# A graph network on one core: the first half of each gate's Wq product moved to the head of the gate, and the gate's end taken bank by bank

## What is computed

```python
def _rgcn(x, W_rel, W_root, bias, src, dst, etype):      # out = x @ W_root + bias
    ...                                                  # + sum over 3 relations of mean(x[src] @ W_rel[r]) by dst
def _gate(h, q, Wg, bg, Wq, bq):
    hg = einsum('bnf,gf->bng', h3, Wg[:, :F]);  qg = einsum('blf,gf->blg', q, Wg[:, F:]) + bg
    attn = sigmoid(hg[:, :, None, :] + qg[:, None, :, :])
    qi = einsum('bnlf,blf->bnf', attn, q)
    alpha = sigmoid(einsum('bnf,gf->bng', h3, Wq[:, :F]) + einsum('bnf,gf->bng', qi, Wq[:, F:]) + bq)
    return alpha * tanh(qi) + (1.0 - alpha) * h3
h = gate(relu(rgcn1(x)));  h = gate(relu(rgcn2(h)));  x = layernorm(x + h)
```

## Time and profile before

| | |
|---|---|
| median of 3 runs | 1258.62 us (1258.33 to 1262.88) |
| the profiled execution | 1258.37 us, its span 1256.6 us |
| PE busy | 1118.9 us, 89% of the span |
| DVE, ACT, POOL busy | 733.8, 548.8, 131.6 us |
| mean granted clock of PE | 0.944 |

### The profile page before, as it was taken

How to read it: one execution, slowest core, us unless ns; L and a number is a source line. 1 busy time by engine, 2 the same in 40 slices (tenths; PEclk the granted TensorE clock), 3 DMA queues, 4 the chain that set the end, 5 groups by cost and what they waited for, 6 DMA issues and landing times. The chain is left out here.

```text
span 1256.6 us, 17142 instructions
## 1 busy us (share of the span) xinstructions
PE 1118.9 (89%) x7246; PEld 921.1 (73%) x7246; DVE 733.8 (58%) x1049; ACT 548.8 (44%) x575; POOL 131.6 (10%) x84
## 2 busy tenths in 40 slices
PE   7999997999879869999579887878999999999986
PEld 6888874445779745448458787854899999999973
DVE  6583447887043158881343464324688888888851
ACT  0221017886032258880123353222566666666630
POOL 2020003554000015550000000000000000000000
PEclk9999997999979989999799888968999999999998
DMA  8044235220323451212224202410877777777720
GB/s 266 1 150 150 76 109 150 61 68 18 118 108 119 136 148 51 66 37 76 76 76 151 76 1 76 173 50 1 272 256 241 248 234 255 233 258 232 257 79 26
DMA packets 82192, 162.66 MB, mean 129 GB/s; under 512 B 4034, under 2 KB 60126, under 8 KB 81822
## 3 DMA queue, kind: packets, MB, share of 16 engines
q1 hardware_dynamic: 80720, 151.86, 36.2%
q0 software_dynamic: 1392, 9.66, 2.9%
HBM read 157.86 MB, written 0.80 MB: 126 GB/s over the span
## 5 line engine op out<-in xcount | busy, mean ns | idle before, releaser
L1533 DVE TENSOR_TENSOR Wlo<-W,Whi 128x2304 fp32r<-128x2304 f32 x68 | 173.7, 2556 | 43.4 <-ACT Whi L1134 43.4
L1134 ACT CAST Whi<-W 128x2304 fp32r<-128x2304 f32 x68 | 144.2, 2122 | 0.0
L851 PE MATMUL PS<-Whi,Mhi 128*128 128x384 f32 x408 | 139.6, 342 | 3.5 <-DVE Mlo L1562 3.5
L618 PE MATMUL PS<-QH,SEL 128*128 128x512 f32 x384 | 118.7, 433 | 23.0 <-DVE QH L1324 15.3
L851 PE MATMUL PS<-Wlo,Mhi 128*128 128x384 f32 x408 | 136.5, 335 | 0.0
L851 PE MATMUL PS<-Whi,Mlo 128*128 128x384 f32 x408 | 136.5, 335 | 0.0
L392 POOL TENSOR_TENSOR PRDP<-arena 128x1024 f32<-128x1024 f32 x48 | 114.5, 2386 | 103.2 <-PE PS L634 83.6
L618 PEld LDWEIGHTS PS<-QH,SEL 128*128 128x128 f32 x384 | 67.4, 195 | 74.2 <-DVE PRD L1348 22.7
L1015 ACT ACTIVATE arena<-PS 128x1024 f32<-128x1024 f32 x96 | 98.5, 1026 | 34.5 <-PE PS L618 34.5
L1015 ACT ACTIVATE PS<-PS 128x1024 f32<-128x1024 f32 x96 | 97.9, 1020 | 0.0
L851 PEld LDWEIGHTS PS<-Whi,Mhi 128*128 128x128 f32 x408 | 76.8, 188 | 8.3 <-DVE Mlo L1562 8.3
(11 more groups left out here) (233 smaller groups left out, 2186.4 us busy)
## 6 DMA issues: line engine op xcount, KB each, us to landing
W<-in_L_rel SPq DMA_DIRECT2D x68, 1152.0 KB, 5.6
W<-in_W_rel SPq DMA_DIRECT2D x6, 2304.0 KB, 8.7
W<-in_W SPq DMA_DIRECT2D x6, 2304.0 KB, 8.4
arena<-in_qU SPq DMA_DIRECT2D x96, 128.0 KB, 2.6
W<-in_WqT SPq DMA_DIRECT2D x4, 2304.0 KB, 9.1
W<-in_W_root SPq DMA_DIRECT2D x2, 2304.0 KB, 14.0
W<-in_WgT SPq DMA_DIRECT2D x2, 2304.0 KB, 8.4
QH<-QH POOLq DMA_DIRECT2D x2, 1536.0 KB, 9.9
```

The lines of the kernel that those rows point to most:

```text
L618: mm = pe.matmul(PS[:, 2 * (c % 3) + b // 2, :], SEL[:, i, :], QH[h][:, u, b:b + 2, :].rearrange("p b f -> p (b f)"), start=True, stop=True)
L851: mm = pe.matmul(PS[:, 4 + s % 2, 0:HALF], MS[a][mb][:, k, j * P:(j + 1) * P], WS[b][w % 3][:, k, :], start=n == 0, stop=n == 17)
L1134: nc.scalar.copy(WS[0][w % 3][:], W[(FIRST34 + r) % 2][:, :, q * HALF:(q + 1) * HALF]).then_inc(w_hi, 1)
L1533: V.tensor_tensor(WS[1][w % 3][:], W[(FIRST34 + r) % 2][:, :, q * HALF:(q + 1) * HALF], WS[0][w % 3][:].bitcast(F32), ALU.subtract).then_i ...
```

## The change

1. PE multiplies hT by Wq's first half right behind `natural3` (and the sort), into banks 0 to 2, while ACT and DVE copy the node rows. ACT copies the result by bank to hqT, in xT's memory; the first two `sums` wait for these copies. After the loop six matmuls with the identity put hqT into banks 3 to 5, and only the product with qiT is left there. SP issues the later queries ahead of m = 9 and 16.
2. Relu, messages, qiT, tanh, sigmoid, multiply, add and the split of hT are done by bank (j = 0, 1, 2), each with its own count; products take the contractions in the order in which the banks come (`ready`).
3. The transposes back to natural form are made in three parts (`turn_part`) in banks 6, 7 and 5: for g = 0 the first inside the last product, the second behind it, the third inside the first product of layer 2. For g = 1 the half statistics follow each addition.
4. ACT and DVE split the first two weight thirds of layer 2 during the gate's last product. qiT gets memory of its own.

```diff
-        alphaT = view(arena, 7936, 1536).rearrange("p (k n) -> p k n", k=KC)
+        alphaT = hqT = xT[:]
...
-                if m in (8, 15):
+                if m in (9, 16):
...
                     for k in range(KC):
+                        if ready and m == 0 and k % 2 == 0:
+                            ready(k // 2)
...
+                    if bank_sem and m in (1, 3):
+                        mm.then_inc(bank_sem, 1)
...
+                    for ks in ((0, 1, 2, 3), (4, 5)) if q == 0 else (range(KC),):
+                        for c in range(2):
+                            for k in ks:
+                                if q == 0 and c == 0 and k % 2 == 0:
+                                    if p == 0:
+                                        pe.wait_ge(hs_ready, k // 2 + 1)
+                                    else:
+                                        pe.wait_ge(mt_copied, 3 * (R3 + p - 1) + k // 2 + 1)
...
-                    pe.wait_ge(mt_copied, 3 * (n + 1))
...
-                pe.wait_ge(relu_done, g + 1)
...
-                natural3(hT, W[(m0 + 4) % 2], bank=3, first=True, last=True).then_inc(w_used, 1)
+                natural3(hT, W[(m0 + 4) % 2], bank=3, first=True, last=True,
+                         ready=lambda j: pe.wait_ge(relu_done, 3 * g + j + 1)).then_inc(w_used, 1)
                 if g == 0:
                     sort_edges()
+                weights(m0 + 5)
+                turned_product(0, hT, W[(m0 + 5) % 2], bank_sem=hq_done).then_inc(w_used, 1)
...
+                    if c < 2:
+                        pe.wait_ge(hq_copied, 3 * g + 2 + c)
...
+                for m in range(KC):
+                    pe.matmul(PS[:, 3 + m // 2, (m % 2) * NODES:(m % 2 + 1) * NODES], ident[:], hqT[:, m, :],
+                              start=m % 2 == 0, stop=False, skip_group_check=True)
                 pe.wait_ge(qi_copied, UNITS * (g + 1))
                 to_turned(0, qiN).then_inc(qi_turned, 1)
-                weights(m0 + 5)
-                turned_product(3, hT, W[(m0 + 5) % 2], last=False).then_inc(w_used, 1)
-                pe.wait_ge(qiT_copied, g + 1)
                 weights(m0 + 6)
-                turned_product(3, qiT, W[(m0 + 6) % 2], first=False).then_inc(w_used, 1)
-                pe.wait_ge(gate_done, g + 1)
-                to_natural(0, hT).then_inc(h_turned, 1)
...
+                turned_product(3, qiT, W[(m0 + 6) % 2], first=False, between=first_part, bank_sem=aq_done,
+                               ready=lambda j: pe.wait_ge(qiT_copied, 3 * g + j + 1)).then_inc(w_used, 1)
+                pe.wait_ge(gate_part, 3 * g + 2)
+                turn_part(1).then_inc(part_turned, 1)
+                if g == 1:
+                    pe.wait_ge(gate_part, 6)
+                    turn_part(2).then_inc(part_turned, 1)
...
+                for j in range(3):
+                    if j < 2:
+                        act.wait_ge(hq_done, 2 * g + j + 1)
+                    else:
+                        act.wait_ge(w_used, 7 * g + 7)
+                    nc.scalar.copy(hqT[:, 2 * j:2 * j + 2, :], PS[:, j, :].rearrange("p (k n) -> p k n", k=2)).then_inc(hq_copied, 1)
...
+                if g == 0:
+                    third_hi_turned(0)
+                    third_hi_turned(1)
...
+                    if g == 0:
+                        act.wait_ge(gate_part, j + 1)
+                        nc.scalar.copy(TS[0][:, 2 * j:2 * j + 2, :], hT[:, 2 * j:2 * j + 2, :]).then_inc(hs_hi, 1)
...
                     third_lo_turned(0)
                     third_lo_turned(1)
+                for j in range(3):
+                    ks = slice(2 * j, 2 * j + 2)
+                    dve.wait_ge(alpha_done, 3 * g + j + 1)
+                    then(V.tensor_tensor(tanhT[:, ks], tanhT[:, ks], alphaT[:, ks], ALU.mult))
+                    V.tensor_tensor(hT[:, ks, :], hT[:, ks, :], tanhT[:, ks], ALU.add).then_inc(gate_part, 1)
+                    if g == 0:
+                        dve.wait_ge(hs_hi, j + 1)
+                        V.tensor_tensor(TS[1][:, ks, :], hT[:, ks, :], TS[0][:, ks, :].bitcast(F32), ALU.subtract).then_inc(hs_ready, 1)
...
+                    dve.wait_ge(part_turned, 3)
+                    for t in range(NT):
+                        then(V.tensor_tensor(xN[:, t, 0:512], PS[:, 6 + t, :], xN[:, t, 0:512], ALU.add))
+                        V.bn_stats(stats[:, t, 0, :], xN[:, t, 0:HALF])
```

More of the change, by code:

```diff
@@ L138, in build @@
         QD = [view(arena, 12032 + 1024 * i, 1024) for i in range(2)]
[L139 to L140 removed]
+        qiT, tanhT = put("qiT", [P, KC, NODES], F32, 100)[:], MT[0][:]
+        alphaT = hqT = xT[:]
         qiN = hN
@@ L412, in natural, with turned_product @@
                 return mm
-            def turned_product(bank, T, Wm, first=True, last=True, between=None):
+            def turned_product(bank, T, Wm, first=True, last=True, between=None, ready=None, bank_sem=None):
                 for m in range(KC):
@@ L464, in spread_counts, with natural3 @@
                 mm.then_inc(deg_spread, 1)
-            def natural3(T, Wm, bank=0, first=False, last=False, tiles=range(NT), thirds=range(3)):
+            def natural3(T, Wm, bank=0, first=False, last=False, tiles=range(NT), thirds=range(3), ready=None):
                 for t in tiles:
@@ L472, in natural3 @@
                         for k in range(KC):
+                            if ready and at == 0 and k % 2 == 0:
+                                ready(k // 2)
                             mm = pe.matmul(out, T[:, k, t * P:(t + 1) * P], Wm[:, k, q * THIRD:(q + 1) * THIRD],
@@ L533, in split_product @@
                     pe.wait_ge(wl_ready, w + 1)
[L534 to L538, removed]
+                    for ks in ((0, 1, 2, 3), (4, 5)) if q == 0 else (range(KC),):
[6 more added lines that the diff above has]
+                                        pe.wait_ge(mt_copied, 3 * (R3 + p - 1) + k // 2 + 1)
+                                for a, b in ((0, 0), (1, 0), (0, 1)):
+                                    mm = pe.matmul(PS[:, q, c * NODES:(c + 1) * NODES], WL[b][w % 2][:, k, c, :], TS[a][:, k, :],
+                                                   start=p == 0 and k == 0 and a == b == 0 and c == 0,
+                                                   stop=p == R3 and k == KC - 1 and b == 1 and c == 1, skip_group_check=True)
                     mm.then_inc(wl_used, 1)
+                    if q == 0 and after_first:
+                        after_first()
             for g in range(2):
@@ L992, in _ @@
                     act.wait_ge(small_in, SMALL)
[L993 to L998, removed]
+                    act.wait_ge(rows_looked, EC // 2)
+                for j in range(3):
+                    if g:
+                        act.wait_ge(wl_used, 3 * R3 + j + 1)
+                    elif j < 2:
+                        act.wait_ge(bank_done, j + 1)
+                    else:
+                        act.wait_ge(w_used, 5)
+                    for m in (2 * j, 2 * j + 1):
+                        ins = nc.scalar.activation(hT[:, m, :], PS[:, j, (m % 2) * NODES:(m % 2 + 1) * NODES], ACT.Relu,
+                                                   bias=biasT[:, g, m:m + 1])
+                    ins.then_inc(relu_done, 1)
                 act.wait_ge(w_used, 7 * g + 6)
@@ L1371, in _ @@
-                if g == 0:
-                    ins.then_inc(hN_ready, 1)
+                for j in range(3):
+                    V.tensor_copy(qiT[:, 2 * j:2 * j + 2, :], PS[:, j, :].rearrange("p (k n) -> p k n", k=2)).then_inc(qiT_copied, 1)
+                for j in range(3):
+                    ks = slice(2 * j, 2 * j + 2)
+                    dve.wait_ge(tanh_done, 3 * g + j + 1)
+                    then(V.tensor_tensor(tanhT[:, ks], tanhT[:, ks], hT[:, ks, :], ALU.subtract))
+                if g == 0:
@@ new lines, in _ @@
+                rest = PS[:, 5, :].rearrange("p (t f) -> p t f", t=NT)
+                if g == 0:
+                    dve.wait_ge(part_turned, 1)
+                    for t in range(NT):
+                        V.tensor_copy(hN[:, t, 0:512], PS[:, 6 + t, :])
+                    dve.wait_ge(part_turned, 2)
+                    V.tensor_copy(hN[:, :, 512:FEAT], rest).then_inc(hN_ready, 1)
+                else:
+                    dve.wait_ge(part_turned, 3)
+                    for t in range(NT):
+                        then(V.tensor_tensor(xN[:, t, 0:512], PS[:, 6 + t, :], xN[:, t, 0:512], ALU.add))
+                        V.bn_stats(stats[:, t, 0, :], xN[:, t, 0:HALF])
+                    dve.wait_ge(part_turned, 4)
+                    then(V.tensor_tensor(xN[:, :, 512:FEAT], rest, xN[:, :, 512:FEAT], ALU.add))
+                    for t in range(NT):
+                        ins = V.bn_stats(stats[:, t, 1, :], xN[:, t, HALF:FEAT])
+                    then(ins)
```

85 lines of the change are left out of this document (39 added, 46 removed).

## The result

Four runs of the changed kernel took 1214.09 to 1222.06 us, median 1218.04, against 1260.75 (1258.33 to 1266.79, four runs) of the kernel before: ratio 0.9654, 95% interval 0.9625 to 0.9684. The profiled execution took 1219.05 us with a span of 1217.3, so 39.3 us less span than before, where 43.4 were forecast. PE is as long busy as before (1118.9 us before, 1118.6 after), with the twelve identity matmuls more; what went is time in which it stood still, and some in which it ran at the low clock.

What follows compares the result with a forecast made beforehand. It took the touched stages to be bound by TensorE plus the places where it stands still, with the low clock behind idle time. Its terms summed to -43.4 us, from 1258.4 to 1215.0 us, range 1208 to 1227.

Steps and rivals of the forecast that it cites:

- (a): Layer 1: relation products started bank by bank hide three 0.68 us waits for the last message copy; -2.0 us.
- (b): Gate 1: relu by bank removes the 2.45 us wait before the node product; -2.5 us.
- (c): Head of gate 1: first-half product +9.0, exposed table load +0.7, warm loop start -1.7; +8.0 us in all.
- (i): Head of gate 2: first-half product +7.0, earlier first sigmoid -0.5, faster loop start -0.95; +5.6 us in all.
- (d): Gate ends: six identity matmuls put hqT back into the accumulators; +2.1 us per gate, 4.2 in all.
- (e): Gate ends, qi transposes to end of products: 31.1 us becomes 16.9; -14.2 us per gate, 28.4 in all.
- (f): Gate 1, end of products to layer 2's first aggregation: 28.3 us becomes 14.3, with a 0.35 us wait; -14.0 us.
- (j): End of gate 2, end of products to aggregate of row statistics: 12.83 us becomes 6.7; -6.1 us.
- the first: Rival: weight conversions become the bound at the gate's end and in layer 2; +7 us, 1222 us; chance 0.14.
- The second: Rival: a head does not absorb the product, weights or node rows late; up to 8.67 us lost, 1224; chance 0.08.
- The third: Rival: better than the sum, identity matmuls at transposes' pace and less start-up in the loops; 1209 us; chance 0.06.
- the fourth: Rival: low clock in the gate loop, one loop some 100 us longer; 1315 us; chance 0.03.

Runs made afterwards that it cites:

- p2: Changed kernel with whole waits in the two layers (message copies, layer product before relu, relu before node product); 1229.75 us, ratio to before 0.9758.
- p5: Changed kernel with added matmuls nobody reads where PE idles at the start of both gate loops; 1215.15 us, ratio to before 0.9661.
- p6: Changed kernel with six unread matmuls between gate 2's last transposes and the transposes ahead of the GCN block; 1216.60 us, ratio to before 0.9652.
- p10: Changed kernel with early table load, unread matmuls at loop starts and gate 2's end, and hqT added by DVE; 1206.32 us, ratio to before 0.9584.
- p1: Changed kernel with Wq's first-half product back behind the loop, steps by bank kept; 1235.78 us, ratio to before 0.9798.
- p4: Changed kernel with a one-column sigmoid ahead of gate 1's hqT copies, loading the activation table early; 1220.25 us, ratio to before 0.9667.
- p7: Changed kernel without the six identity matmuls, DVE adding hqT to each bank instead; 1215.67 us, ratio to before 0.9648.
- p8: Changed kernel with the first-half product back behind the loop and layer 2's first two weight thirds converted behind the gate's parts; 1236.13 us, single run.
- p3: Changed kernel with whole waits at the gates' ends, same pieces (qiT copies, sigmoids, parts, transposes, split of hT); 1235.10 us, ratio to before 0.9804.
- p9: Changed kernel with whole waits both in the two layers and at the gates' ends; 1248.55 us, ratio to before 0.9903.

## Why the prediction was right, and where it was off

The forecast was 1215.0 with a range of 1208 to 1227; measured 1218.04. The sum of -43.4 stands against -39.3 in the spans. Two pieces of the table cover several terms, since a whole relu or a set of six sigmoids ends later by itself than a last pair (1.46 us).

- (a), (b), layer 1 by bank: -4.5 forecast, -4.9 measured (4.14 + 0.72). With whole waits (p2) the first comes back as 4.17; of the 2.29 in the second some 1.6 are a cold start that the kernel before didn't have there.
- (c), (i), the product at the heads: +9.7 and +6.5 to the first sigmoid forecast (15.7 less the idle time, with the table load in one and not in the other), +9.61 and +6.13 measured.
- (c), (i), the loop's start: **this step failed.** "In return PE comes warm into the loop: 8.8 instead of 10.49" gave -1.7 and -0.95; measured -0.38 and +0.51. PE did come warm, but the loop's own first waits let the clock fall. The gain of 1.7 and 1.6 was there, as p5 shows, where added matmuls kept the clock up. I had taken the idle time ahead of the loop for the only cause of the low clock in it.
- (d), (e), gate ends: +2.1 - 14.2 forecast, -12.1 a gate; measured 39.17 to 25.74, -13.43, of which 1.46 are the shorter last set: -12.0, in both gates.
- (f): -14.0 forecast, -12.46 - 1.46 = -13.9 measured. The one wait foreseen, 0.35 us, was 0.45 (the prediction's terms for part 3, 0.85 + 2 x 0.73 + 0.63 + 0.73, make 3.67 and not the 3.75 it gives, so 0.27 by its own sum).
- (g), (h), layer 2: -8.2 forecast, -6.46 - 2.76 = -9.2 measured. The waits of 1.40 were worth 1.67 each (aggregations 19.81 us apart before, 18.14 or 18.13 after).
- (j): -6.1 forecast, -5.03 - 1.46 = -6.5 measured.
- Not in the sum: +2.2 us of the GCN product, which started cold; p6 and p10 show it to be the clock. It was cold in all seven kernels with the gate's end by bank and no matmuls added there (the changed one, p1, p2, p4, p5, p7, p8: 23.7 to 24.5 us to its end) and warm before and in p3 and p9, which have whole waits there (21.98 or 21.99). So it comes with the steps by bank and takes 2.2 back from them; why the clock is still low there is not shown. And +0.83 at the start of the kernel, ahead of the change, a matter of the run.

So 2.8 us at the loops' starts, 2.2 at the GCN block and 0.8 at the front were missed, and 1.7 gained in small parts, which brought the sum nearer than its terms were. Of the rivals, the first did not come: in all of layer 2 PE has only the wait of 0.45 us, for hT's low part, and none for a weight third. The second did not come, in spite of the shared transfers: no DMA wait stands at gate 2's ninth step any more. The third did not come either: the identity matmuls took 2.69 us (312.50 to 315.19), not the transposes' 1.5, and the loops' starts gave nothing. Nor did the fifth. For the fourth, of the swing between the two levels, the windows of the changed kernel show it at both loop starts, 3 to 4 us long each and not through the loop (1.00 from 216 to 300 us). The Trainium skill, TensorE: Matmul & The Clock Gate, section A second HAM failure mode: psum-queue depth-cycling, tells of small idle times between groups of matmuls and a clock that swings between its levels. The trace agrees for the first steps, with one fall at each loop's start behind idle times of 1.14 and 1.76 or of 1.86 us, and not for the loop's body. I had weighed it for the whole loop only and dismissed it by a window of 100 us, in which those few microseconds hide.

The table load: the Trainium skill, ScalarE: Activation LUTs, section What ACT_TABLE_LOAD costs, has 1283 ns and a drain of about 1380. The trace has 1.28 us and the first sigmoid 0.02 us behind it, and taking the load off the path gave 1.41 us, not 2.66. No drain is seen on this path.

The split of the gain, by experiments: steps by bank in the layers 14.1 us (p2), steps by bank at the gates' ends 19.8 (p3, of which some 3.4 are the two cold last products), and the rest, the moved product with the early conversions that it makes possible, 9.0 by itself (p9). Together 42.9, against 42.6 in the table (518.7 to 476.1). With all else in place the move is worth 16.8 there (p1; 17.7 of the span), and the steps by bank 25.8 without it and 33.6 with it. The parts by bank and the moved product need each other: with the product back at the tail, the early conversions stand in ACT's way.

## What to carry to other kernels

Where a product needs nothing from the stage ahead of it, put it where the critical engine waits for copies, and price it as its length less the idle time, plus what it takes to bring the result back. When a weight's last use moves earlier, look at which load it frees and what can start on it: here over 40% of the move's worth lay there (7.3 to 7.6 of 17.7 us). Look at the granted clock in windows of a microsecond or two at the seams of the stages, not over a stage: a few matmuls nobody reads, in waits of 1 to 2 us, gave 3.1 us back. And look one stage past the change: the GCN product, which nothing touched, took 2.2 us longer.

## What was not expected of the hardware

The granted clock fell behind waits as short as 1.14 and 1.76 us (PE busy 0.00 and 0.37 us in the two windows before the fall), and behind 1.86 us in gate 2; in p7, whose loop start has the same instructions, it stayed at 1.00 in gate 2 behind 1.85 us (8.70 us to the ninth sigmoid) and fell in gate 1. A node product behind 2.4 us of idle time was cold in gate 2 before (17.38 us) and warm in gate 1 (15.8), the other way round in p2, and cold in both in p9. So the same code behind the same wait can be warm or cold, some 1.6 us a place. What decides it no run here shows.

The stretch behind the GCN product, where no experiment changed anything, took from 617.66 (p2) to 624.96 us (p4) in the profiled executions. Cut from the product's end on, the first three windows of 100 us had granted clocks of 0.83, 0.85 and 0.90 in p4 against 0.86, 0.87 and 0.91 in p2. The runs of the changed kernel go the same way, with a mean granted clock of 0.959 in the shortest (1214.09 us) and 0.950 in the longest (1222.06); that their difference lies in this stretch is likely and not shown. What decides the clock there was not tried.
